# Feed-forward block with a 4-bit activation: the residual is stored ahead and the quantised values are added to it in the output by accumulating transfers

## The reference, cut to what matters

```python
x = x + xattn(layernorm(x), ctx, ctx, ...)     # cross attention
x = x + attn(layernorm(x), ...)                # differential attention, 8 heads
h = gelu(layernorm(x) @ ternary(W1).T + b1)    # 4096 hidden units
y = h @ ternary(W2).T + b2
scale = max(abs(y)) / 7 + 1e-8                 # one maximum over the whole of y
q = clip(round(y / scale), -7, 7) * scale
out = x + q                                    # 1024 rows (16*64) of 1024 float32
```

## Time and profile before

| | us |
|---|---|
| median of 3 runs | 1598.61 (1597.87 to 1599.70) |
| the profiled execution, its own time | 1598.41 |
| its span, first to last instruction | 1596.6 |
| PE busy | 1496.6 (94% of the span) |
| last matmul ends | about 1571 |
| maximum known, scale ready | 1573.7 |
| first store of the output issued | 1583.08 |
| last DVE instruction ends | 1591.6 |

### The profile page before, as it was taken

The page is one execution under the profiler, slowest core; times in us unless marked ns, Lnnn a source line. Parts: engine busy times, 40 slices in busy tenths (PEclk is TensorE's granted clock), DMA queues, the critical chain, the costliest instruction groups (busy, mean ns, idle before and its releaser), DMA issues.

```text
span 1596.6 us, 19216 instructions
## 1 busy us (share of the span) xinstructions
PE 1496.6 (94%) x7948; PEld 778.3 (49%) x7948; DVE 828.8 (52%) x1359; ACT 348.9 (22%) x558; POOL 11.7 (1%) x12
## 2 busy tenths in 40 slices
PE   6899999999999849899999999799899999999993
PEld 3444535445454425576666667444344444444441
DVE  3544646455465567888888888443333333002007
ACT  2221313223141122333333333100212221000002
POOL 0000000000000000000000000000000000000002
PEclk9999999999999979999999999999999999999997
DMA  9998989989898744556555554000211111111102
GB/s 338 334 390 323 385 320 343 338 305 394 311 353 316 272 176 158 179 165 192 174 159 169 153 146 130 1 0 0 47 40 40 40 35 54 40 37 41 37 30 105
DMA packets 132326, 282.22 MB, mean 177 GB/s; under 512 B 40832, under 2 KB 57472, under 8 KB 132240
## 3 DMA queue, kind: packets, MB, share of 16 engines
q1 hardware_dynamic: 121728, 242.72, 44.3%
q10 hardware_dynamic: 10512, 38.28, 6.7%
HBM read 252.14 MB, written 28.84 MB: 176 GB/s over the span
## 4 chain that ended last, share of the span: by engine, by line
PE 77%; DVE 9%; DMA 8%; issue 2%; SPq 2%; ACT 1%; DVEq 0%; POOL 0%
PE ps L904 14%; PE ps L917 14%; PE ps L735 11%; PE ps L665 7%; PE ps L857 7%; PE ps L781 7%; PE ps L680 7%; DMA t_dram<-t_out 4%; PE ps L632 3%; PE ps L831 3%; SPq L296 2%; DMA ctxT<-in_ctx0T 1%; DVE t_out L1138 1%; PE ps L745 1%; PE ps L721 1%
## 5 line engine op out<-in xcount | busy, mean ns | idle before, releaser
L781 PE MATMUL ps<-x2T,wqkv_sb 128*128 128x512 f32 x512 | 223.6, 597 | 7.2 <-DVE v_sb L1198 5.5
L917 PE MATMUL ps<-t_half,h_hi 128*128 128x512 f16 x512 | 194.3, 379 | 0.0
L917 PE MATMUL ps<-t_half,h_lo 128*128 128x512 f16 x512 | 194.1, 379 | 0.0
L735 PE MATMUL ps<-ctx_sb,attnT 128*64 128x512 f32 (+1 forms) x832 | 181.8, 597 | 0.0
L781 PEld LDWEIGHTS ps<-x2T,wqkv_sb 128*128 128x128 f32 x512 | 97.3, 192 | 127.1 <-issue 126.7
L904 PE MATMUL ps<-x3h,t_buf 128*128 128x512 f16 x512 | 153.6, 382 | 3.5 <-DMA t_buf<-t_dram 3.5
L904 PE MATMUL ps<-x3l,t_buf 128*128 128x512 f16 x512 | 153.4, 382 | 0.0
L665 PEld LDWEIGHTS ps<-cst,ctx_sb 128*128 128x128 f32 x1024 | 109.9, 141 | 54.9 <-issue 36.9
L665 PE MATMUL ps<-cst,ctx_sb 128*128 128x128 f32 x1024 | 130.3, 280 | 3.3 <-DMA ctx_sb<-in_ctx 3.3
L472 ACT ACTIVATE ctxT<-ps 128x512 f32<-128x512 f32 (+1 forms) x160 | 88.8, 579 | 188.6 <-PE ps L665 170.1
L995 DVE COPY ctxT<-ps 128x512 f32<-128x512 f32 (+1 forms) x128 | 82.3, 656 | 86.4 <-PE ps L665 68.9
(11 more groups left out here) (177 smaller groups left out, 1352.0 us busy)
## 6 DMA issues: line engine op xcount, KB each, us to landing
ctx_sb<-in_ctx SPq DMA_DIRECT2D x44, 2048.0 KB, 18.0
ctxT<-in_ctx0T SPq DMA_DIRECT2D x14, 2048.0 KB, 22.7
wa_buf<-in_w2t ACTq DMA_DIRECT2D x32, 512.0 KB, 4.4
w_buf<-in_w1t SPq DMA_DIRECT2D x32, 512.0 KB, 4.0
t_dram<-t_out SPq DMA_DIRECT2D x64, 256.0 KB, 4.3
w_buf<-in_w2t SPq DMA_DIRECT2D x32, 512.0 KB, 4.0
wa_buf<-in_w1t ACTq DMA_DIRECT2D x28, 512.0 KB, 7.7
wqkv_sb<-in_wqkv SPq DMA_DIRECT2D x24, 512.0 KB, 5.0
```

The costliest lines, as they stand in the source:

```text
L735: ins = mm(bank(2 + hf)[C * b:C * b + C, :], attnT[0:w, mt, C * b:C * b + C], ctx_sb[0:w, b, mt, hf * BANK:hf * BANK + BANK], start=(mt == ...
L781: ins = mm(bank(b0 + hf), wqkv_sb[:, w, c, :], x2T[:, c, hf * BANK:hf * BANK + BANK], start=(c == 0), stop=(c == NC - 1))
L917: ins = mm(bank(t), part[:, hc, t * P:t * P + P], t_half[:, hc % 8, :], start=(hc == 0 and n == 0), stop=(hc == HC - 1 and n == 1))
```

## The change

Behind the load of b2 and ahead of the refills of `t_half`, SP stores the 8 tiles of the residual `xo` to the output. In the tail, `xo` is no longer used. DVE takes ROUND off and multiplies by the scale in one instruction for every one of the 8 tiles. POOL, after its all-reduce, waits until the 8 stores have landed, and then issues for each tile, as soon as DVE has finished it, a transfer from `y` to the output that adds (`accum_op=ALU.add`) what it carries to what stands there. ACT keeps its 7 roundings and loses the two instructions of line 609. SP's last act is to wait until the 8 accumulating transfers have landed.

```diff
@@ sync
             sp.wait_ge(h_ready, 2 * HC + 2)
             sp.dma_start(b2_bc[:, :], b2.partition_broadcast(P)).then_inc(b2_in, 16)
+            for t in range(NT):
+                sp.dma_start(out_v[:, t, :], xo[:, t, :]).then_inc(out_stored, 16)
             for n in range(8, 2 * HC):
...
-            n_vec = 0
-            for t in range(NT):
-                if t in Q_POOL:
-                    sp.wait_ge(pool_ready, Q_POOL.index(t) + 1)
-                    sp.dma_start(out_v[:, t, :], xo[:, t, :]).then_inc(out_stored, 16)
-                    continue
-                for f in [slice(0, N)] if t < NT - 1 else [slice(0, BANK), slice(BANK, N)]:
-                    n_vec += 1
-                    sp.wait_ge(q_ready, n_vec)
-                    sp.dma_start(out_v[:, t, f], xo[:, t, f]).then_inc(out_stored, 16)
-            sp.wait_ge(out_stored, 16 * (NT + 1))
+            sp.wait_ge(q_stored, 16 * NT)
@@ gpsimd
             pool.partition_all_reduce(ym[:, 17:18], ym[:, 16:17], P, RED.max).then_inc(y_all, 1)
-            for n, t in enumerate(Q_POOL):
-                pool.wait_ge(scaled_ready, n + 1)
-                pool.tensor_tensor(xo[:, t, :], xo[:, t, :], y[:, t, :], ALU.add).then_inc(pool_ready, 1)
+            pool.wait_ge(out_stored, 16 * NT)
+            for t in range(NT):
+                pool.wait_ge(scaled_ready, t + 1)
+                pool.dma_start(out_v[:, t, :], y[:, t, :], accum_op=ALU.add).then_inc(q_stored, 16)
@@ scalar
-            def whole(t):
-                act.wait_ge(z_ready, t)
-                A(y[:, t, :], y[:, t, :], ACT.Copy, bias=-ROUND).then_inc(whole_ready, 1)
-
             for t in range(1, NT):
                 rounded(t)
-                if t in Q_ACT:
-                    whole(t)
@@ vector
-                if t in Q_POOL:
-                    V.tensor_scalar(y[:, t, :], y[:, t, :], -ROUND, ym[:, 19:20], ALU.add, ALU.mult)\
-                        .then_inc(scaled_ready, 1)
-                    continue
-                if t in Q_ACT:
-                    V.wait_ge(whole_ready, Q_ACT.index(t) + 1)
-                else:
-                    own.done(V.tensor_scalar(y[:, t, :], y[:, t, :], -ROUND, None, ALU.add))
-                for f in [slice(0, N)] if t < NT - 1 else [slice(0, BANK), slice(BANK, N)]:
-                    V.scalar_tensor_tensor(xo[:, t, f], y[:, t, f], ym[:, 19:20], xo[:, t, f], ALU.mult, ALU.add)\
-                        .then_inc(q_ready, 1)
+                V.tensor_scalar(y[:, t, :], y[:, t, :], -ROUND, ym[:, 19:20], ALU.add, ALU.mult).then_inc(scaled_ready, 1)
```

More of the change, by code:

```diff
@@ L62 @@
 QMAX = 7.0
-Q_POOL = (0, 2, 4)
-Q_ACT = (3, 6)
 C_ID, C_PAIR, C_MASK, C_ONE, C_W = 0, P, 2 * P, 2 * P + D, 2 * P + D + P
@@ L240, in build @@
         t2_used, y_done, y_out, y_max, y_all = sem("t2_used"), sem("y_done"), sem("y_out"), sem("y_max"), sem("y_all")
-        scaled_ready, whole_ready, pool_ready = sem("scaled_ready"), sem("whole_ready"), sem("pool_ready")
-        z_ready, q_ready, d_vec, out_stored = sem("z_ready"), sem("q_ready"), sem("d_vec"), sem("out_stored")
+        scaled_ready, q_stored = sem("scaled_ready"), sem("q_stored")
+        z_ready, d_vec, out_stored = sem("z_ready"), sem("d_vec"), sem("out_stored")
         def apart(eng):
```

## The result

Twelve runs of each kernel give a median of 1602.4 us for the changed one (1598.78 to 1604.55) and 1597.83 us for the one before; the ratio is 1.0026, with a 95% interval of 1.0017 to 1.0035. The change costs about 4.2 us by the ratio (4.6 by the two medians). The interval excludes 1, but it holds the 0.2% (1.0020) that the prediction took as the bound from which a difference can be told. The forecast was 1601, 2.5 us above before.

What follows compares the result with a forecast made beforehand. PE bounds the kernel up to the last matmul, then the tail's DMA transfers: first data 1577.2 + 21.0 for eight + 0.9 = span 1599.1, 2.5 above 1596.6, so a time of 1601; range 1589.5 to 1612.

Steps and rivals of the forecast that it cites:

- The doubled transfer: Tail, DMA engines: an accumulating transfer makes two reads in turn, 2.62 us a tile against 1.31 plain, 21.0 us for eight.
- the ends 1.31 and 3.93: Tail, us per accumulating tile: 1.31 if the second read runs beside the first, 3.93 if two reads and write take turns.
- A (1.31): Rival for the tail's transfers: the addition is free, 1.31 us a tile, 8.0 us less, a time of 1591; chance 0.26.
- B (3.93): Rival for the tail's transfers: reads and write don't overlap, 3.93 us a tile, 12.9 us more, time 1612; chance 0.20.
- The early start: Start of the tail's transfers: first data at 1577.2 instead of 1583.9, 6.7 us gained.
- POOL's issues following each other without a pause: Tail, POOL: the forecast is wrong if its issues, not the transfers, follow each other without a pause; issue taken 0.35 us.
- Rival C: Tail: POOL issues late, held off by DVE or a code change; 8.5 us more, time 1607 (or 1605.4); chance 0.13.
- the 5.1 us before: Tail of the kernel before: POOL's first addition starts 5.1 us after its input, read as a change of POOL's code.
- The early stores: SP queue, start of second product: 8 stores ahead of the refills, cost 0, 9 us left before PE needs chunk 8.
- ACT and DVE: Tail: ACT's last rounding ends at 1581.2, DVE's last scaling at 1582.0; worth nothing if transfers need longer than 1.05 us each.
- The term that was too small: End of the tail: 0.9 us from the last data to the end of the span.

Runs made afterwards that it cites:

- e1_plain: The changed kernel with POOL's 8 transfers as plain stores of y, without the addition: 1591.05 us, ratio 0.9963 to the kernel before.
- e4_four: The changed kernel with POOL's first 4 transfers accumulating and the last 4 plain stores: 1597.67 us, ratio 0.9997 to the kernel before.
- e6_f16: The changed kernel with quantised values written as float16 and added to the float32 output by the same 8 transfers: 1598.41 us, ratio 0.9995 to the kernel before.
- e5_code: The changed kernel with one 128x1 POOL addition between its all-reduce and its transfers: 1606.8 us, ratio 1.0068 to the kernel before.
- e2_no_early: The changed kernel without the 8 early stores of the residual and POOL's wait for them: 1601.46 us, ratio 1.0039 to the kernel before.

## Why the prediction came out as it did

- **The doubled transfer** was the term that decided. Taken 2.62 us a tile, measured 2.54 in the full stretches; 21.0 us for the eight, measured 20.8 with the slow start (below). The choice between the ends 1.31 and 3.93 was right: e1_plain and e4_four show that the addition doubles the transfer, and e6_f16 that the price goes by bytes read. That fits the reason given, that a second read finds no free channel; the channels themselves no row shows. Rivals A (1.31) and B (3.93) fall.
- **The early start.** First data was expected 3.5 us after the scale, and came after about 3.8. From tile 0 ready (1573.05) to data (about 1575.3) 2.2 us pass, against 0.35 + 0.8 + 0.75 = 1.9. They divide into 0.63 until the first issue starts (1573.68; taken 0.75), 1.02 for the issue (taken 0.35) and about 0.6 from its end to data (taken 0.8). That the sum nearly holds is in part luck: the issue was taken at a third of its length, the other two parts too long. The eight issues take 1.02 to 1.91 us by their records and overlap, in 7.91 us together; DVE's step of 1.04 sets their pace there. In e5_code, where most tiles were ready, eight took 7.40, 0.93 each. Against 2.54 for a transfer, the later issues are covered. The prediction named POOL's issues following each other without a pause as a sign against it. They do so until 1581.6, but so do the transfers, for 14 us longer, and these set the end.
- **Rival C** (POOL late, held off by DVE or by the change of code) falls on both counts: no pair of MODIFY_POOL_CONFIG comes before a transfer, and POOL's issues keep up with DVE's step of 1.04 us. The prediction's reading that the 5.1 us before were not DVE's doing is shown by e5_code.
- **The early stores** were costed at 0, with 9 us to spare at chunk 8: right, by the matmuls without idle time and by e2_no_early. SP took 8.6 us for the eight issues, within the 2.7 to 9.6 given.
- **ACT and DVE**: expected to end 7.5 and 8.3 us after the scale, ended at 7.4 and 8.2; worth nothing, as said.
- **The term that was too small** is the last: 0.9 us from the last data to the end, carried over from SP's stores. After the bulk of the data ends (1596.1) a remnant goes on until about 1597.2, at times a single row of 4 KB in 0.2 us (the row 1596.80), and the span ends 2.3 us after the bulk. That is 1.4 us too little; with 0.3 more for the early start and 0.2 less for the transfers the forecast of +2.5 becomes +4.0, against 4.0 in the traces and 4.2 by the ratio. Plain stores issued by POOL have 1.3, so about 1 us belongs to the addition; why a few rows come late wasn't examined.

The forecast named no difference that can be told, with a lean to slower; the ratio lies on that side, and its interval holds the bound. The step the prediction didn't take was to ask what the plain way would give if POOL were left out: it had the delay of 5.1 us in hand, and the removal of POOL alone gains 5.5 us in the tail, where the change loses 4.0. Only a free addition would have gained more (7.2 us, by the tail of e1_plain).

## What to carry to other kernels

Count an accumulating transfer by the bytes it reads: the destination is read as well, so it takes the DMA engines about twice a plain store when both sides are float32. In a tail that those engines already bound it doesn't pay; whether it does where they are idle no run here shows. Where an engine starts late though its input was ready, look in its queue for what stands ahead of the instruction before blaming the one named as releaser; here POOL's first addition behind its all-reduce started 7 us after it, 5.1 us after its input was ready, and giving the three additions to DVE gained 0.3%.

## What was not expected

**POOL's issue beside DVE.** In e1_plain, where the issues show apart, timelines of DVE and POOL:

```profile
1578.29 0.75 DVE L1284 TENSOR_SCALAR y<-y,ym 128x1024 f32<-128x1024 f32 x1 [0.29 <-ACT y L596]
1579.33 0.75 DVE L1284 TENSOR_SCALAR y<-y,ym 128x1024 f32<-128x1024 f32 x1 [0.29 <-ACT y L596]
...
1578.30 0.86 POOL L432 DMA_DIRECT2D out<-y  x1 [0.18 <-issue]
1579.34 0.86 POOL L432 DMA_DIRECT2D out<-y  x1 [0.18 <-issue]
1580.38 0.53 POOL L432 DMA_DIRECT2D out<-y  x1 [0.18 <-issue]
...
1576.03 0.53 POOL L432 DMA_DIRECT2D out<-y  x1
1576.21 0.87 DVE L1284 TENSOR_SCALAR y<-y,ym 128x1024 f32<-128x1024 f32 x1 [0.29 <-ACT y L596]
```

The two issues that begin with an instruction of DVE take 0.86 us and end 0.12 us after it; the last, with DVE idle, takes 0.53. This fits an issue that waits for DVE's instruction to end, at a price of 0.33 us each; it was not tested by itself. The Trainium skill (SBUF — State Buffer, "A bandwidth-pool intuition that's wrong (but worth ruling out)") has it as blocked until VectorE's end plus about 115 ns, and these rows agree. One issue of this kernel does not wait: it starts at 1576.03, 0.18 us ahead of a DVE instruction, and takes 0.53, while that instruction takes 0.87 us instead of 0.75. So the one that comes first goes first, as far as one case shows. The starvation that rival C feared is then real but small, since each instruction of DVE is short.

**A slow first stretch.** In the changed kernel the us from 1575 and 1576 show shares of 1.09 and 0.80 at 98 and 147 GB/s, where the later ones move 207. Counted from 1575.2, when the first data moves, that is 0.6 to 0.7 of the later pace, while the records count the engines as nearly or fully busy. The cause was not examined.
